# All lower drives of a state-space scan on TensorE, one C product in four on GpSimd, and a re-placed order of side work

## What is computed

```python
# 256 inner channels, 16 states, once forward and once on the flipped sequence
def step(h, ins):
    dt_t, u_t, B_t, C_t = ins
    h = jnp.exp(dt_t[..., None] * A) * h + (dt_t * u_t)[..., None] * B_t[:, None, :]
    y_t = jnp.einsum('bdn,bn->bd', h, C_t)
    return (h, y_t)
y = jnp.moveaxis(ys, 0, 1) + u * Dp
y = y * jax.nn.silu(z)
# attention, 16 heads over 4 key heads, 8 features a head
scores = jnp.einsum('bhqd,bhkd->bhqk', q, k) / np.sqrt(HD)
scores = jnp.where(mask, scores, -1e+30)
probs = jax.nn.softmax(scores, axis=-1)
```

## Time and profile before

| | |
|---|---|
| median of 3 runs | 802.06 us (799.94 to 804.38) |
| the profiled execution | 804.5 us, its span 802.7 us |
| scan loop, first scan to end of the last C product | 108.6 to 529.3 us |
| busy over the span: TensorE, VectorE, ScalarE, GpSimd | 676.3, 586.0, 535.1, 416.6 us |
| DMA | 99.5 MB in all, 195 GB/s in the loop |

### The profile page before, as it was taken

One profiled execution on the slowest core, in us unless ns is written; L12 is line 12 of the kernel. 1 busy time (PEld: TensorE's weight loads), 2 busy tenths in 40 slices (PEclk: granted clock), 3 DMA queues, 4 the chain that ended last, 5 costly groups with the idle time before them and its releaser, 6 DMA issues.

```text
span 802.7 us, 13340 instructions
## 1 busy us (share of the span) xinstructions
PE 676.3 (84%) x4403; PEld 491.5 (61%) x4403; DVE 586.0 (73%) x863; ACT 535.1 (67%) x1021; POOL 416.6 (52%) x362
## 2 busy tenths in 40 slices
PE   5899968888988887988969876698888888888986
PEld 3588837666676675865857666687673343444433
DVE  7435679999989999899989897983435435655532
ACT  4364577868768686787787885735637657766563
POOL 6301078998989989889998897730000000000000
PEclk8799999999899997999979978899999999999998
DMA  5324558577595785755858768800200000000000
GB/s 168 106 80 132 162 159 214 169 203 208 182 243 165 174 236 176 205 185 168 233 166 203 193 178 229 249 1 27 79 2 0 1 1 2 1 2 1 14 14 27
DMA packets 80963, 99.54 MB, mean 124 GB/s; under 512 B 32496, under 2 KB 37624, under 8 KB 80896
## 3 DMA queue, kind: packets, MB, share of 16 engines
q1 hardware_dynamic: 80896, 98.70, 43.4%
HBM read 96.05 MB, written 2.72 MB: 123 GB/s over the span
## 4 chain that ended last, share of the span: by engine, by line
PE 42%; DVE 17%; ACT 15%; issue 14%; POOL 8%; DMA 3%; DVEq 0%; POOLq 0%; SPq 0%; ACTq 0%
POOL drive L648 5%; DVE ps L1161 4%; PE ps L1772 4%; PE ps L2064 3%; DVE moe L1161 3%; PE ps L1823 3%; PE ps L1838 3%; POOL hc L656 3%; PE ps L2033 3%; ACT ps L851 2%; PE ps L2041 2%; PE ps L1907 2%; PE ps L1702 2%; DVE hc L1169 2%; PE ps L2071 2%
## 5 line engine op out<-in xcount | busy, mean ns | idle before, releaser
L648 POOL TENSOR_TENSOR drive<-dtu,b_sb 128x512 f32<-128x512 f32 x160 | 202.6, 1274 | 6.0 <-DMA b_sb<-bc_rows 5.9
L656 POOL TENSOR_TENSOR hc<-moe,c_sb 128x512 f32<-128x512 f32 x128 | 162.9, 1273 | 26.6 <-DVE moe L1161 26.5
L1161 DVE TENSOR_TENSOR_SCAN moe<-ps,drive 128x512 f32<-128x512 f32 x128 | 153.5, 1199 | 0.2 <-POOL hc L656 0.2
L1772 PE MATMUL ps<-ident,hc 128*128 128x128 f32 x1024 | 147.5, 293 | 0.6 <-POOL hc L656 0.6
L1772 PEld LDWEIGHTS ps<-ident,hc 128*128 128x128 f32 x1024 | 129.8, 153 | 25.8 <-issue 24.8
L1161 DVE TENSOR_TENSOR_SCAN ps<-decay_sb,ps 128x512 f32<-128x512 f32 x96 | 117.3, 1222 | 29.0 <-ACT ps L851 14.4
L1068 ACT ACTIVATE probs<-ps 128x1024 f32<-128x1024 f32 (+1 forms) x96 | 87.6, 914 | 67.4 <-PE ps L2041 57.0
L851 ACT ACTIVATE ps<-dt,negA 128x510 f32<-128x510 f32 x160 | 105.7, 676 | 14.9 <-DVE moe L1161 11.0
L661 POOL TENSOR_TENSOR stat<-stat,halfc 128x4 f32<-128x4 f32 x7 | 7.0, 1007 | 193.4 <-DVE stat L1426 193.4
L1169 DVE TENSOR_TENSOR hc<-ps,c_sb 128x512 f32<-128x512 f32 x128 | 85.3, 666 | 0.0
L1750 PE MATMUL ps<-xm,dtuT 128*128 128x128 f32 x384 | 59.6, 305 | 14.8 <-DMA xm<-spot_rows 8.4
(11 more groups left out here) (281 smaller groups left out, 1231.0 us busy)
## 6 DMA issues: line engine op xcount, KB each, us to landing
b_sb<-bc_rows SPq DMA_DIRECT2D x128, 256.0 KB, 4.1
c_sb<-bc_rows SPq DMA_DIRECT2D x128, 256.0 KB, 4.5
xm<-spot_rows SPq DMA_DIRECT2D x48, 256.0 KB, 3.8
wbuf<-in_pack SPq DMA_DIRECT2D x16, 514.0 KB, 3.4
wbuf<-in_pack SPq DMA_DIRECT2D x8, 512.0 KB, 3.5
x_sb<-in_x SPq DMA_DIRECT2D x4, 256.0 KB, 3.6
spot_rows<-c_sb SPq DMA_DIRECT2D x4, 256.0 KB, 4.6
out<-x_sb SPq DMA_DIRECT2D x4, 256.0 KB, 2.3
```

What stands on the lines that cost most here:

```text
L648: pool.tensor_tensor(drive_of(N, half), dtu[:, N // STATES % 2, half], b_sb[:, N % B_RING], ALU.mult) \
L656: pool.tensor_tensor(hc[:, 2 * (N % DEEP) + half], h_of(q), c_sb[:, N % C_RING], ALU.mult).then_inc(sem["hc_pooled"], 1)
L1161: dve.tensor_tensor_scan(h_of(q)[:, turn], decay_bank(q)[:, turn], source[:, turn], 0.0, ALU.mult, ALU.add).then_inc(sem["scan_done"], 1)
L1772: last = pe.matmul(ps[:, Y_BANK + half, block], hc[:, 2 * (N % DEEP) + half, block], ident[:], start=False, stop=True, is_transpose=True, ...
```

## The change

Nothing of what is computed changes.

- **Drives.** All lower drives are made by TensorE; `drive_half` becomes `drive_upper`. State 0 of each group joins the spots (7 states by spots, 9 scaled). Spots are stored five states ahead of their state, in six rows of HBM in place of four, and loaded one state earlier; for state 0 store and load stand as before.
- **C products.** For N with N % 4 == 1 (`lent`) the lower scan writes to an SBUF buffer `h_lent`, and GpSimd multiplies it by C ahead of its upper product.
- **Buffers.** Lower results have three PSUM banks; decays have two banks in PSUM (upper) and two buffers in SBUF (lower): a decay waits for the scan two states before. `dtuT` and `bT` are doubled. For the backward direction the boundary columns are cleared one by one behind the scans that free them, not all together.
- **Order.** ScalarE copies u half 1, both y and both z one state later; the slots of TensorE stay. z's second half is copied plain, then Silu runs on u and on all of z. dt stands at slots 9 and 11, t at 13, b at 14. The norms of layer 1 go from groups 5, 6, 7 into groups 6 and 7, the transposes `xt` all into group 7.
- **Transfers.** The loads of layer 1's tables, now 15, go from state 116 to state 126 on the Sync queue, the experts behind the loop.
- **Masks.** Each mask matmul of 128 rows and 128 columns becomes two of 64 rows and 64 columns; the second head of a unit uses the other two quadrants of the array, with a copy of the mask whose halves are swapped.

```diff
-OWN_H = 2
+OWN_H = 3
-SPOT_AT = (5, 6, 7, 9, 10, 13)
-SPOT_ROWS, SPOT_RING = 4, 3
+SPOT_AT = (0, 5, 6, 7, 9, 10, 13)
+SPOT_ROWS, SPOT_RING, SPOT_LEAD = 6, 3, 5
...
-                          10: [("dt", n, 0)], 12: [("dt", n, 1)], 14: [("b", n)], 15: [("t", n)]})
+                          9: [("dt", n, 0)], 11: [("dt", n, 1)], 13: [("t", n)], 14: [("b", n)]})
...
-            slots.update({14: [("xt", g - PAIRS - 1)], 15: [("logits", 0)]})
-        elif g > PAIRS:
-            slots[14] = [("xt", g - PAIRS - 1)] + slots[14]
+            slots.update({9: [("xt", 0)], 11: [("xt", 1)], 14: [("xt", 2)], 15: [("logits", 0)]})
...
-        for kind, j, evs in (("y", 4, [("y", g - 1, 0)]), ("y", 5, [("y", g - 1, 1)]), ("z", 6, [("z", g + 1, 0)]), ("z", 7, [("z", g + 1, 1)])):
+        for kind, j, evs in (("y", 5, [("y", g - 1, 0)]), ("y", 6, [("y", g - 1, 1)]), ("z", 7, [("z", g + 1, 0)]), ("z", 8, [("z", g + 1, 1)])):
...
+    for g in range(STEPS - 1):
+        rest.remove(("u", g + 1, 1))
+        rest.insert(rest.index(("state", g * STATES + 4)) + 1, ("u", g + 1, 1))
...
+    for g, j, ev in ((6, 3, ("n", 0, 0)), (6, 5, ("n", 0, 1)), (6, 14, ("n", 0, 2)),
+                     (7, 1, ("n", 1, 0)), (7, 2, ("n", 1, 1)), (7, 4, ("n", 1, 2)), (7, 6, ("rms", 0)), (7, 8, ("rms", 1)),
+                     (7, 10, ("n", 2, 0)), (7, 11, ("n", 2, 1)), (7, 13, ("n", 2, 2))):
+        rest.insert(rest.index(("state", g * STATES + j)), ev)
...
+def lent(N):
+
+    return N % 4 == 1
...
+DECAYS = 2
...
 def decay_before(q):
 
+    return q - HALVES * DECAYS
...
-                if N == ALL - STATES + 4:
+                if N == ALL - 2:
                     load_l1()
-                for e in range(RING):
-                    if N == ALL - 10 + 2 * e:
-                        load_expert(e)
-            for e in range(RING, EXPERTS):
+            for e in range(EXPERTS):
                 load_expert(e)
...
                     if N:
+                        if lent(N - 1):
+                            times_c(N - 1, 0)
                         times_c(N - 1, 1)
                     if M < ALL:
-                        drive_half(M, 1)
+                        drive_upper(M)
...
-                    act.activation(z_s[:, g % 2, 1], side, ACT.Silu).then_inc(sem["side_free"], 1)
-                    act.wait_ge(sem["side_free"], SIDE["z", g, 0] + 1)
-                    act.activation(z_s[:, g % 2, 0], z_s[:, g % 2, 0], ACT.Silu).then_inc(sem["z_ready"], 1)
-                    act.wait_ge(sem["side_free"], SIDE["u", g, HALVES - 1] + 1)
+                    act.activation(z_s[:, g % 2, 1], side, ACT.Copy).then_inc(sem["side_free"], 1)
                     act.activation(u_s[:, g % 2], u_s[:, g % 2], ACT.Silu).then_inc(sem["u_ready"], 1)
+                    act.wait_ge(sem["side_free"], SIDE["z", g, 1] + 1)
+                    act.activation(z_s[:, g % 2], z_s[:, g % 2], ACT.Silu).then_inc(sem["z_ready"], 1)
                     act.preload_act_table_set("natural_log_exp_and_others")
...
-                after(pe, "hc_ready", N - OWN_H + 1)
+                before = N - OWN_H
+                if before >= 0 and lent(before):
+                    pe.wait_ge(sem["scan_done"], HALVES * before + 1)
+                elif before >= 0:
+                    pe.wait_ge(sem["hc_ready"], own_before(HALVES * before) + 1)
...
-                    if ev[1] + 1 < ALL and turned(ev[1] + 1):
+                    if ev[1] == 0:
+                        turn_drive(0)
+                    if ev[1] + 1 < ALL:
                         turn_drive(ev[1] + 1)
...
-                        pe.matmul(ps[:, kv], ident16[:], masks[:, l].unsqueeze(1).broadcast_to([P, GROUP, P]),
-                                  start=True, stop=False)
+                        for rows in HALF_ROWS:
+                            keys = rows if kv == kvs[0] else HALF_ROWS[rows is HALF_ROWS[0]]
+                            pe.matmul(ps[keys, kv], ident16[rows, rows],
+                                      masks[rows, l if kv == kvs[0] else 3 + l].unsqueeze(1).broadcast_to([P // 2, GROUP, P]),
+                                      start=True, stop=False)
```

More of the change, by code:

```diff
@@ L268, with lent_before, zero_rank @@
 PREP = {ev: n for n, ev in enumerate(ev for ev in FILL + AT_ORDER if ev[0] in ("T", "L", "Q", "K", "O1", "O2"))}
+def lent(N):
+    return N % 4 == 1
+def lent_before(N):
+    return (N + 2) // 4
 def shared_before(q):
-    return q // HALVES
+    N, half = divmod(q, HALVES)
+    return N + lent_before(N) + (half and lent(N))
 def own_before(q):
[L278 to L287, removed]
+    N, half = divmod(q, HALVES)
+    return N - lent_before(N) + (half and not lent(N))
 def by_spots(N):
     return N % STATES in SPOT_AT
-SPOTS = [N for N in range(ALL) if turned(N) and by_spots(N)]
-SCALED = [N for N in range(ALL) if turned(N) and not by_spots(N)]
-assert all(turned(N) for N in SPOT_AT)
+SPOTS = [N for N in range(ALL) if by_spots(N)]
+SCALED = [N for N in range(ALL) if not by_spots(N)]
 def scaled_before(N):
     return sum(n < N for n in SCALED)
[L305 to L318, removed]
+DECAYS = 2
 def decay_before(q):
[L323 to L328, removed]
+    return q - HALVES * DECAYS
+FIRST_USE = [range(start, start + HALVES * DECAYS) for start in (0, BACKWARD)]
+def zero_rank(back, q):
+    return FIRST_USE[back].index(q)
 def build(nc, a, out):
@@ L420, in build @@
         rope_k = sb("rope_k", [P, 2, 2, GT * KV * HD])
-        masks = sb("masks", [P, 3, P], F16)
+        masks = sb("masks", [P, 5, P], F16)
         ident16 = sb("ident16", [P, P], F16)
@@ L702, in _ @@
                         pool.wait_ge(sem["dtu_ready"], HALVES)
+                        pool.wait_ge(sem["e0_down"], PAIRS0)
                         for first in range(DRIVES - 1):
-                            for half in range(HALVES):
-                                if half or first and not turned(first):
-                                    drive_half(first, half)
+                            drive_upper(first)
                     M = N + DRIVES - 1
@@ L1174, in zero_boundary, with turn_boundary @@
                     .then_inc(sem["zero_cols"], 1)
+            def turn_boundary(before):
+                for q in FIRST_USE[1]:
+                    if decay_before(q) == before:
+                        dve.wait_ge(sem["scan_done"], before + 1)
+                        zero_boundary(q, SEQ - 1)
             def state(N):
@@ L1184, in state @@
                 scan(N, 1)
-                if last:
-                    for q in FIRST_USE[1]:
-                        dve.wait_ge(sem["scan_done"], decay_before(q) + 1)
-                        zero_boundary(q, SEQ - 1)
-                times_c(N)
+                turn_boundary(2 * N + 1)
+                if not lent(N):
+                    times_c(N)
             def gate_y(g):
@@ L1749, in turn_drive @@
                     if by_spots(N):
-                        last = pe.matmul(ps[:, H_BANKS[N % OWN_H], block], dtuT[:, block], spots[:, n % SPOT_RING, block], start=True, stop=True)
+                        last = pe.matmul(turned_bank(N)[:, block], dtuT[:, N // STATES % 2, block], spots[:, n % SPOT_RING, block], start=True, stop=True)
                     else:
-                        last = pe.transpose(ps[:, H_BANKS[N % OWN_H], block], scaled[:, n % 2, block], ident[:])
+                        last = pe.transpose(turned_bank(N)[:, block], scaled[:, n % 2, block], ident[:])
                 last.then_inc(sem["drive_turned"], 1)
```

107 lines of the change are left out of this document (52 added, 55 removed).

## The result

The changed kernel takes **857.2 us** (median of four runs, 854.4 to 861.5) where the kernel before takes 801.5: a ratio of 1.070, 95% interval 1.064 to 1.076. The forecast was 800.5, with 815 as its upper end. The profiled execution took 854.4 us around a span of 852.4.

A forecast was written before the change was run, and what follows sets the result against it. In plain groups of the loop VectorE ends last, GpSimd close behind, with little to spare elsewhere. Loop terms of +4.4 us and masks of -6 gave -1.6 from the 802.06 us median: 800.5 us, range 778 to 815.

The forecast's parts named there:

- the second rival: Loop: TensorE stands still for copies and state 0's spots, then taps run at 1.2 GHz; 813 us, chance 0.17.
- The late spots: Group's end: TensorE waits for state 0's spots; no term in the sum, only named in the second rival.
- State 4 behind y: Plain groups: state 4's turned drive behind y comes 1.8 us late; states 0 to 4's start +1.3 us.
- group 3's +2.3: Forecast change of group 3, a plain group taken at 52.6 us: 2.3 us longer.
- The copies: ScalarE's y and z copies a state later: states 4 and 5 take 7.5 us, +1.0; states 6 to 9 +0.9.
- States 6 to 9: Plain group: later z copy and table loads make these states take 14.0 us where they took 13.1, +0.9.
- States 10 to 15: Plain group: two C products moved win 1.1 us, of which GpSimd's dtu may take 0.7.
- The half clock: TensorE's taps meeting a 1.2 GHz stretch, 2 us more in six groups; part of the second rival, not the sum.
- The start: Group 0: state 0's drive behind two taps puts the first scan at 110.9, not 108.6, +2.3 us.
- The masks: Attention: mask matmuls in quadrants save TensorE time, six tenths of which arrive; 4 to 8 us, taken as -6.
- The third rival: Attention: quadrants of one bank don't run together, +8 us in place of -6; 814 us, chance 0.12.
- The first rival: Loop: both chains cost nothing, since ScalarE and TensorE have more lead than forecast; 775 us, chance 0.24.

The follow-up runs named there:

- e1: Changed kernel with state 0's spots, and the B and C rows ahead of them, stored and loaded earlier on the Sync queue; 833.2 us, ratio 1.040.
- e2: e1 with the copies of u half 1, y and z back at the states where the kernel before has them; 803.2 us, ratio 1.004.
- e5: e2 with the turned drives of states 4 and 5 ahead of y's transposes, and at the start state 0's ahead of the taps; 789.7 us.
- e6: e5 with the masks as in the kernel before, one matmul of 128 rows instead of two of 64; 786.6 us, ratio 0.981.
- e3: Changed kernel with only the copies of u, y and z back at the old places, state 0's spots still late; 833.8 us, ratio 1.042.
- e7: e5 with the copies of u, y and z a state later, as in the changed kernel; 805.9 us, ratio 1.004.
- e4: Kernel before with the quadrant masks and their two loads, nothing else; 805.6 us, ratio 1.006.
- e9: Kernel before without its 128 mask matmuls, so the diagonal blocks aren't masked; 794.7 us, ratio 0.992.

## Why the prediction was wrong

Nearly every sign that the prediction named came: states 4 and 5 at 7.8 us (9.5 in groups 2 and 6), TensorE's wait of 2.69 us ahead of z half 0, the first scan at 110.85, masks to keys at 0.35 us. The sign for the second rival, a clock below 0.85, did not. None of them looked at the group's end.

The parts of the loss, in the order in which the runs took them away: 24.0 us the late spots (changed kernel to e1), 30.0 the late copies (to e2), 13.5 the turned drives of states 0, 4 and 5 (to e5), 3.1 the masks (to e6), which then lies 13.9 under the kernel before. 24.0 + 30.0 + 13.5 + 3.1 - 13.9 = 56.7, for 55.7 measured. The order matters, since the losses don't add. Over e2 the late spots alone cost 30.6 (e3) and the late copies alone 30.0 (e1), but both together 54.0: one wait hides part of the other. Over e5 the late turned drives alone cost 13.5 (e2) and the late copies alone 16.2 (e7), but both together 43.5 (e1): there one makes the other dearer.

- **The late spots: the step that failed.** The sum had no term for them. The prediction knew the wait ("at the group's end for the spots of state 0") but put it among the rivals, as a risk that a stretch at half clock brings, with 2 us a group. They cost 24 to 32 us, 3.4 to 4.6 a boundary. It could have been worked out: the queue is in program order, the rows' store stands behind a C row that waits for GpSimd (272.35 in the changed kernel), and behind it come two landings in HBM and a load, 13.5 us from 272.72 to 286.22, while TensorE wanted the spots at 281.60, 8.9 us after the rows' store was issued. I had followed the Sync queue past the copies and the experts, but not along the chain store, landing, store, landing, load that the change puts ahead of state 0. Before, that chain ended in a B row for GpSimd, without its last two links.
- **State 4 behind y: right at full clock.** +1.3 us for states 0 to 4's start (its own terms, 1.8 less one product of 0.58, give 1.2, as group 3's +2.3 is 2.0 from 50.6 to 52.6); e1 has 2.82 + 2.24 + 2.81 + 5.91 = 13.78 in group 1, before 12.50 in group 3. In three of e1's six groups it is 7.56 instead of 5.91, and those 1.65 us had no term.
- **The copies: right in mechanism, too small.** Their terms, +1.0 and +0.9 us a group, are 11 us in six groups; the late copies cost 16.2 to 30.0. Forecast were 7.5 us for states 4 and 5; 7.8 at full clock (e7), 9.2 to 9.5 in five of e1's six groups. With the copies as before they take 5.1 (e2) or 5.6 to 6.5 (e5 outside group 1), so +1.0 against before hid a loss of more than 2.
- **States 6 to 9, 14.0 us:** 14.17. But with the copies as before it is 13.80 to 13.87, so the cause that I named, the copies, carries 0.3 to 0.4 of the 1.1 us; the rest I haven't tested.
- **States 10 to 15:** forecast 0.4 us less; e1 is 0.6 less in group 3 up to the start of state 15, then 0.3 more (3.57 for 3.29); in groups 1 and 2 it is 1.0 less, then 0.9 more.
- **The half clock as a rival only.** It decides "from one such stretch a group", I wrote, and it does: beyond the steps above, five groups of e1 hold stretches at 1.2 GHz worth 1.6 to 3.2 us each. e1's loop is 23.6 us longer than before's to the last scan, where the sum without the start had +2.1. This should have been part of the forecast, as TensorE was to stand still in two places a group by the forecast's own words, for 2.5 us in the first.
- **The start:** first scan at 110.85, forecast 110.9. With state 0's turn behind the taps it came at 110.9 to 114.2, with the turn ahead of them at 108.3 to 111.5, and in the traces of the kernel before, e4 and e9, which don't touch it, at 108.6 to 110.1. With such a scatter the hit is in part luck.
- **The masks: nothing gained.** -6 forecast; +4.8 (1.4 to 7.7) in e4, and between e5 and e6 3.1 that the scatter could give. The way of 0.35 us was inside the forecast's 0.32 to 0.43, the six tenths wrong. A share of the chain (10.2% in the earlier trace rows) says through which work the chain went, not what its removal gives: e9 removes 34 us of which that chain held 20.7, and 6.3 arrive.
- **The third rival, quadrants of one bank in turn,** is refuted by those 0.35 us. The Trainium skill, "TensorEngine Tiling (Array Packing)", Restrictions and Gotchas, has row tiles that cannot use one PSUM bank at the same time; here two 64-row tiles write the two halves of one bank's partitions, and the measurement decides: the second of two old mask matmuls starts 0.2 us behind the first (the two last 0.59 us, one 0.38), while four in quadrants last 0.41 and one of them 0.40.
- **The first rival, 775 us,** was not reached; e6, the change with its order mended and the old masks, has the lowest median of all runs, 786.6, 1.9% under the kernel before.

On the fixed part of a DMA the Trainium skill ("DMA: Bandwidth & Descriptors", Anatomy of one DMA) gives about 2 us of set-up and completion for a DMA that GpSimd issues; these were issued by Sync. The rows here took 3.3 us to land, the spots 5.2 (512 elements, each to a place of its own) and the 256 KB load 4.1. As an estimate by that page, the three fixed parts would be 6 of these 12.5 us; no run here separates them.

## What to carry to other kernels

When a value gets a new maker, follow its inputs backwards through every queue, issue by issue, with the landing times of the profile, and compare the sum with the lead that the queue has: here three landings and a queue's place came to 13.5 us. TensorE's clock fell behind many of its waits here, and two of them within a few states cost more than their sum (43.5 us for 29.7); put its next independent work (here the turned drives) into the wait, which turned a kernel 0.4% slower than before into one 1.4% faster. And a share of the chain of waits is at best an upper bound of what its removal gives: take the work out once, as in e9, before reshaping it.

## What the runs showed of the hardware

- The same wait of 2.69 us was followed by TensorE at 2.4 GHz in one group of a run and at 1.2 GHz in the next (e1: the turned drive by eight matmuls 1.06 and 1.92 us). In e2 the sixteen diagonal matmuls took 2.05 or 3.67 us behind waits of 1.71 and 1.97.
- Four mask matmuls of 64 rows and 64 columns, each with 512 columns streamed, took 0.35 us to the next kind, two of 128 rows 0.53, with the two halves of one bank written at once.
- A store of 512 single elements from HBM to HBM took 5.2 us to land (median of 56 stores in the changed kernel 5.6), while the queues carried about 165 GB/s; it is the longest link of the chain and moves 2 KB.
